# Two halves of the small products in the extra bank, around the other products of a position

## What is computed

```python
h = take(L0_tok_W.T, x)                          # embedding, vocabulary 4360
h = h + toeplitz_mixer(layernorm(h), ...)        # FFT convolution, gates
h = h + product_key_attention(layernorm(h), ...) # 8 heads, see below
h = h + attention(layernorm(h), Wq, Wk)          # softmax(q k / 8) @ x, one head
h = h + moe(layernorm(h), ...)                   # 8 experts, top 2, exact gelu
```

```python
k = einsum('bnhk,bnhkd->bnhd', kv_scores, keys_table[ind])
v = einsum('bnhk,bnhkd->bnhd', kv_scores, values_table[ind])
attn = softmax(where(causal, einsum('bihd,bjhd->bhij', q, k), neg), -1)
out = einsum('bhij,bjhd->bhid', attn, v) @ Wo
```

## Time and profile before

| | |
|---|---|
| median of three executions | 3286.44 us |
| profiled execution, span | 3919.1 us |
| profiled execution, mean granted TensorE clock | 0.869 |
| PE busy | 2986.0 us, 76% |
| DVE busy | 2791.8 us, 71% |
| ACT busy | 2037.7 us, 52% |
| POOL busy | 2052.1 us, 52% |

### The profile page before, as it was taken

How to read it: one execution, slowest core, us unless ns; L and a number is a source line. 1 busy time by engine, 2 the same in 40 slices (tenths; PEclk the granted TensorE clock), 3 DMA queues, 4 the chain that set the end, 5 groups by cost and what they waited for, 6 DMA issues and landing times. The chain is left out here.

```text
span 3919.1 us, 39389 instructions
## 1 busy us (share of the span) xinstructions
PE 2986.0 (76%) x9782; PEld 1393.2 (36%) x9782; DVE 2791.8 (71%) x9999; ACT 2037.7 (52%) x4498; POOL 2052.1 (52%) x2095
## 2 busy tenths in 40 slices
PE   4861667868786768878787878787878878787888
PEld 2430222424333323334333433333333433333443
DVE  7678777777777777777768786767768887864423
ACT  3231544555555655556555655555555755555522
POOL 3011666566666666565656655555656565655300
PEclk7985777989788989999889989888988989998999
DMA  1001121212121212111111111121211111111000
GB/s 37 22 8 52 45 66 43 59 46 58 48 58 48 58 48 59 45 53 51 54 50 48 56 45 55 41 57 44 58 45 52 53 51 48 47 56 42 23 3 3
DMA packets 85626, 179.86 MB, mean 46 GB/s; under 512 B 40177, under 2 KB 41107, under 8 KB 85398
## 3 DMA queue, kind: packets, MB, share of 16 engines
q0 software_dynamic: 66560, 135.40, 13.2%
q1 hardware_dynamic: 18838, 41.94, 3.4%
HBM read 176.15 MB, written 1.05 MB: 45 GB/s over the span
## 5 line engine op out<-in xcount | busy, mean ns | idle before, releaser
L1356 POOL DMA_INDIRECT mx_G<-in_kv_table,mx_slot_i x2048 | 1998.7, 976 | 1388.0 <-issue 605.7
L1384 PE MATMUL mx_acc<-mx_W,mx_table 128*128 128x512 f32 x2048 | 1179.6, 660 | 3.4 <-ACT mx_kvT L1586 3.2
L1743 DVE SCALAR_TENSOR_TENSOR mx_W<-mx_D,mx_W 128x512 f32<-128x512 f32 x1024 | 698.5, 682 | 352.7 <-ACT mx_W L1579 257.9
L1579 ACT ACTIVATE mx_W<-mx_D 128x512 f32<-128x512 f32 x1024 | 607.5, 594 | 525.0 <-remote 235.1
L1647 ACT ACTIVATE mx_GT<-mx_G,mx_slot_w 128x128 f32<-128x128 f32 x2048 | 759.1, 495 | 3.9 <-DVE mx_KVs L1960 1.9
L1374 PE MATMUL mx_D<-mx_U,mx_pick_b 96*128 96x512 bf16 x1024 | 434.3, 424 | 117.6 <-remote 53.8
L1384 PEld LDWEIGHTS mx_acc<-mx_W,mx_table 128*128 128x128 f32 x2048 | 437.4, 215 | 214.9 <-issue 130.4
L1603 ACT ACTIVATE mx_PT<-mx_area 128x512 f32<-128x512 f32 x480 | 246.7, 516 | 455.1 <-remote 145.2
L1396 PE MATMUL mx_O<-mx_PT,mx_KVs 128*65 128x512 f32 (+3 forms) x768 | 333.2, 517 | 130.7 <-ACT mx_OT L1595 86.7
L1410 PE MATMUL mx_area<-mx_KTa,mx_QTa 64*128 64x512 f32 (+3 forms) x384 | 202.9, 613 | 248.0 <-DVE mx_mx_part L1978 83.0
L1960 DVE TENSOR_REDUCE mx_KVs<-mx_GT 128x128 f32<-128x2048 f32 x128 | 292.0, 2281 | 7.5 <-ACT mx_GT L1647 7.3
(11 more groups left out here) (382 smaller groups left out, 4439.9 us busy)
## 6 DMA issues: line engine op xcount, KB each, us to landing
mx_table<-in_kv_dense SPq DMA_DIRECT2D x64, 512.0 KB
mx_G<-in_kv_table,mx_slot_i POOLq DMA_INDIRECT x2048
tz_table<-in_c_dft SPq DMA_DIRECT2D x1, 2048.0 KB
tz_table<-in_c_idft SPq DMA_DIRECT2D x8, 256.0 KB, 2.6
out_h<-mx_xc SPq DMA_DIRECT2D x4, 256.0 KB
mx_G<-in_c_pick SPq DMA_DIRECT2D x1, 528.0 KB
st_h<-in_tok_W,em_ids POOLq DMA_INDIRECT x32
st_keys<-in_pk_keys SPq DMA_DIRECT2D x1, 512.0 KB, 3.8
```

What stands on the lines that cost most here:

```text
L1356: pool.indirect_dma_start(G[g % RING][:, r, :], None, a["kv_table"], bass.IndirectOffsetOnAxis(slot_i[n % 2][:, k, r:r + 1], 0))\
L1384: pe.matmul(acc[:, :], table[:, tile, :], W[c % TILE_RING][:, :], start=(tile == 0), stop=(tile == TILES - 1)).then_inc(applied, 1)
L1579: act.activation(W[c % TILE_RING][:, :], D_ps[c % 3][:, :], ACT.Exp).then_inc(p_done, 1)
L1743: dve.scalar_tensor_tensor(W[c % TILE_RING][:, :], D_ps[c % 3][:, :], 0.0, W[c % TILE_RING][:, :], ALU.is_ge, ALU.mult).then_inc(w_done, 1)
```

## The change

Five of the uses of the extra bank (U, post, KK, neg, Y) are cut in two. The two waits and the first half of the transposes or products move into `begin_extra`, which runs ahead of the position's other products; the second half stays where it was, and it alone tells that the bank is ready. Where the position has a weigh or an area product, the first half stands behind `apply_dense` and ahead of those; where it has neither, it stands between `score_dense` and `apply_dense`. The other uses keep their place whole. No instruction is added or taken away.

```diff
+            def begin_extra(key):
+                kind, n = key[0], key[1]
+                if kind not in ("U", "post", "KK", "neg", "Y"):
+                    return
+                pe.wait_ge(x_taken, cnt.x[key])
+                if kind == "U":
+                    pe.wait_ge(pc_ready, STEPS * n + key[2] // 2 + 1)
+                    turn_split(key, (0, 1))
...
+            def project_heads(key, parts):
+                head = key[1] % HP + HP * key[2]
+                for j in parts:
+                    last = pe.matmul(X_ps[:, j * (D + 1):(j + 1) * (D + 1)], OT[:, j * P:(j + 1) * P], o_w[:, head, :],
+                                     start=True, stop=True)
+                return last
...
             def fill_extra(key):
-                pe.wait_ge(x_taken, cnt.x[key])
+                if kind not in ("U", "post", "KK", "neg", "Y"):
+                    pe.wait_ge(x_taken, cnt.x[key])
...
                 if kind == "U":
-                    pe.wait_ge(pc_ready, STEPS * n + key[2] // 2 + 1)
-                    flat = X_ps[:, :].bitcast(BF16)
-                    for g in range(4):
...
+                    last = turn_split(key, (2, 3))
...
+                key = cnt.x_at.get(divmod(q, SLOT))
                 late = c % TILES == 0
+                early = bool(area_uses(q - 2)) and area_uses(q - 2)[0] in cnt.weigh or bool(area_uses(q))
+                if key is not None and not early:
+                    begin_extra(key)
                 if 0 <= c < PAIRS * SLOT and not late:
                     apply_dense(c)
+                if key is not None and early:
+                    begin_extra(key)
                 for use in area_uses(q - 2):
                     if use in cnt.weigh:
                         weigh(use)
```

More of the change, by code:

```diff
@@ L1467, in idle_products @@
                               skip_group_check=True)
+            def begin_extra(key):
[6 more added lines that the diff above has]
+                    turn_split(key, (0, 1))
+                if kind == "post":
+                    pe.wait_ge(acc_taken, 2 * n + key[2] + 1)
+                    turn_sums((0, 1))
+                if kind == "KK":
+                    pe.wait_ge(kv_ready, NB * n + 4 * key[2] + 4)
+                    turn_keys(key, (0, 1))
+                if kind == "neg":
+                    if key[2] == 0:
+                        pe.wait_ge(scores_taken, cnt.scored["S", n, 1, 3] + 1)
+                    else:
+                        pe.wait_ge(max_done, 2 * n + 2)
+                    turn_maxima(key, (0, 1))
+                if kind == "Y":
+                    pe.wait_ge(o_taken, cnt.o["ST", n, key[2], key[3]] + 1)
+                    project_heads(key, (0, 1))
@@ new lines, in turn_split, with turn_sums @@
+            def turn_split(key, parts):
+                flat = X_ps[:, :].bitcast(BF16)
+                for g in parts:
+                    for e in range(2):
+                        at = (2 * g + e) * P
+                        last = pe.transpose(flat[0:96, at:at + P], PC[:, key[2] % 2 * 2 + e, g, :, :].rearrange("p a c -> p (a c)"),
+                                            ident_b[:, :])
+                return last
+            def turn_sums(parts):
+                for j in parts:
+                    last = pe.transpose(X_ps[:, j * P:(j + 1) * P], kvT[:, j * P:(j + 1) * P], ident[:, :])
+                return last
@@ new lines, in turn_keys, with turn_maxima @@
+            def turn_keys(key, parts):
+                for j in parts:
+                    last = pe.transpose(X_ps[:, j * P:(j + 1) * P], KV[key[1] % 2][:, 4 * key[2] + j, 0:2 * D], ident[:, :])
+                return last
+            def turn_maxima(key, parts):
+                for j in parts:
+                    last = pe.matmul(X_ps[0:D + 1, j * P:(j + 1) * P], mx[:, key[2], j:j + D + 1], ident[:, :],
+                                     start=True, stop=True)
+                return last
@@ L1483, in fill_extra @@
                 if kind == "U":
-                    pe.wait_ge(pc_ready, STEPS * n + key[2] // 2 + 1)
-                    flat = X_ps[:, :].bitcast(BF16)
-                    for g in range(4):
[L1487 to L1490, removed]
+                    last = turn_split(key, (2, 3))
                 if kind == "post":
-                    pe.wait_ge(acc_taken, 2 * n + key[2] + 1)
-                    for j in range(4):
-                        last = pe.transpose(X_ps[:, j * P:(j + 1) * P], kvT[:, j * P:(j + 1) * P], ident[:, :])
+                    last = turn_sums((2, 3))
                 if kind == "KK":
-                    pe.wait_ge(kv_ready, NB * n + 4 * key[2] + 4)
-                    for j in range(4):
-                        last = pe.transpose(X_ps[:, j * P:(j + 1) * P], KV[n % 2][:, 4 * key[2] + j, 0:2 * D], ident[:, :])
+                    last = turn_keys(key, (2, 3))
                 if kind == "QQ":
@@ L1502, in fill_extra @@
                 if kind == "neg":
[L1503 to L1509, removed]
-                if kind == "Y":
[L1511 to L1515, removed]
+                    last = turn_maxima(key, (2, 3))
+                if kind == "Y":
+                    last = project_heads(key, (2, 3))
                 if kind in ("l1x", "l2x"):
@@ L1566, in _ @@
                         fill_area(use)
-                if divmod(q, SLOT) in cnt.x_at:
-                    fill_extra(cnt.x_at[divmod(q, SLOT)])
+                if key is not None:
+                    fill_extra(key)
                 if 0 <= c < PAIRS * SLOT and late:
```

## The result

| | before | after |
|---|---|---|
| median of the runs | 3286.32 us (4 runs, 3283.16 to 3289.22) | 3309.51 us (4 runs, 3304.64 to 3315.03) |
| ratio, 95% interval | | 1.0062 [1.0049, 1.0075] |

A forecast was written before the change was run, and what follows sets the result against it. Neither engine fills the span: TensorE and VectorE take turns as the bound. Terms 6.9 + 6.9 + 0 + 3.2 + 0 - 3.6 = 13.4 us on 3286.4 gave 3299.8, or 3300 us; range 3275 to 3325 us.

The forecast's parts named there:

- position 6: Second U: the apply would wait for the previous U's copy, 0.86 us in 8 slots without other products; +6.9 us.
- position 5: First U: the apply would wait for VectorE's adds, 0.86 us in 8 slots without other products; +6.9 us.
- position 4: Y: TensorE would wait 0.65 us for the copy of sim in 7 slots, but covered; 0, uncovered 4.6 us.
- position 38: U behind the U of position 37: the score area would start about 0.2 us later in 16 slots; +3.2 us.
- position 26: Half of neg can fill a score area's wait for maxima, 7 us in all, but TensorE has time; 0.
- order within Y: Two runs of four have two short first steps in place of one, 0.06 us for 64 uses; -3.6 us.
- positions 7 to 15: Positions 8, 12 and 13 lie where VectorE is behind; 0, bounded by 13.8 us if ScalarE is late at 13.
- the first half would find the bank free (0): Position 5 with a weigh or area: VectorE's adds end before the weigh starts, so no wait; 0.
- the delay is covered by VectorE's backlog: Position 4: VectorE comes to read Y only after it is through, so TensorE's delay costs 0.
- rival of filled waits: First halves run in area products' waits for maxima at positions 26 and 38; -10.7 us, 3276 us, chance 19%.
- ScalarE's lateness: Copies at 4, 13 and 38 come after the new place, applies and areas lose cover; 3310 to 3343 us, chance 10%.
- The covered waits: At positions 5 and 6 TensorE's lost time comes out of waits it has anyhow; 3286 up to 3293 us, 26%.

The follow-up runs named there:

- cut_456: The changed kernel with uses cut only in positions 4, 5 and 6, whole in the old place elsewhere; 3308.67 us, 1.0059 of before.
- waits_first: The changed kernel with the waits moved ahead but all products of a use in their old place; 3310.12 us, 1.0059 of before.
- second profile of before: The kernel before, unedited, run and profiled again; 3289.38 us, ratio 1.0000, span 3290.5 us.
- cut_5_beside: The changed kernel with uses cut only in position 5 of slots with a weigh or area product there; 3298.81 us, 1.0025 of before.
- cut_beside: The changed kernel with uses cut only in positions with a weigh or area product, whole elsewhere; 3303.07 us, 1.0043 of before.
- cut_alone: The changed kernel with uses cut only in positions without a weigh or area product, whole elsewhere; 3295.74 us, 1.0020 of before.
- cut_dense: The changed kernel with uses cut only in positions 42 to 63, whole in the old place elsewhere; 3286.79 us, 0.9995 of before.
- u_later: The kernel before with the two U of positions 5 and 6 moved whole to 6 and 7; 3279.29 us, 0.9965 of before.
- u_later_all: The kernel before, uses whole, with U of 5 and 6 at 6 and 7, U of 38 at 39, post of 40 at 41; 3282.42 us, 0.9972.

## Why the prediction was right, and where it was right by luck

The forecast was 3300 us, by TensorE's stalls behind moved waits in positions 4 to 6. The time is 3309.5 us, and that mechanism is shown three times: by place (cut_456), by part (waits_first) and in the idle time of the groups. That the number came near is partly luck, as the terms show. The distances, 14 slots, beside the sum's terms for 16:

```
term                     predicted   measured (distances)
position 6                   +6.9        +7.5
position 5                   +6.9       +16.6
position 4                    0          +7.7
position 38                  +3.2        +2.3
position 26                   0         -10.0 (27 to 36: +4.7)
order within Y               -3.6        -2.2 (three Y of four)
positions 7 to 15             0         -11.3
```

**Position 6.** Nearly right. In the slots without other products it lost 5.4 us in 7 of the 8, where 7 x 0.86 = 6.0 were priced; where it took 1.8 us before (slots 2, 3 and 6), it takes 2.7. That nothing is paid in slots where the position has other products was only nearly right too: 2.0 us (3.2 to 3.7 in some).

**Position 5.** The step "the first half would find the bank free (0)" where there is a weigh or an area failed. It rested on one slot, in which the adds ended 0.19 us ahead of the weigh, and that slot was from the disturbed profile. The row itself held the warning: that apply takes 2670.68 - 2668.97 = 1.71 us to the next start, twice the 0.86 that was priced, so the slack was that of an apply at half clock. In the second profile of before, the same slot 12 (PE, then DVE):

```profile
2236.02 1.02 PE L1384 MATMUL mx_acc<-mx_W,mx_table 128*128 128x512 f32 x2
2236.88 1.02 PE L1396 MATMUL mx_O<-mx_PT,mx_x 128*65 128x512 f32 x2
...
2236.85 0.85 DVE L2007 SCALAR_TENSOR_TENSOR st_h<-mx_X,mx_rz,st_h 128x64 f32<-128x64 f32 x4
```

Here the adds end at 2237.70, 0.82 us after the weigh starts. In all eight slots of this kind they end after that place, by 0.2 to 3.4 us. In slot 11 of before, PE from the apply on:

```profile
2068.57 1.02 PE L1384 MATMUL mx_acc<-mx_W,mx_table 128*128 128x512 f32 x2
2069.43 1.02 PE L1440 MATMUL mx_area<-mx_KTl,mx_QTl 128*128 128x512 f32 x2
2070.37 0.65 PE L1489 MATMUL mx_X<-mx_ident_b,mx_PC 128*96 128x128 bf16 x8
```

and of after (PE, then DVE: the last add of the heads):

```profile
2079.10 1.02 PE L1384 MATMUL mx_acc<-mx_W,mx_table 128*128 128x512 f32 x2
2081.04 0.42 PE L1501 MATMUL mx_X<-mx_ident_b,mx_PC 128*96 128x128 bf16 x4 [0.92 <-DVE st_h L2053]
2081.30 1.08 PE L1440 MATMUL mx_area<-mx_KTl,mx_QTl 128*128 128x512 f32 x2
2082.22 0.39 PE L1501 MATMUL mx_X<-mx_ident_b,mx_PC 128*96 128x128 bf16 x4
...
2080.14 0.85 DVE L2053 SCALAR_TENSOR_TENSOR st_h<-mx_X,mx_rz,st_h 128x64 f32<-128x64 f32 x4
```

The adds end at 2080.14 + 0.85 = 2080.99, which is 1.89 us after the start of the apply. The area product, whose data are ready, ran under the adds before; now it starts at 2081.30 in place of some 0.9 us after the apply. The distance of the position grows by 0.9 to 1.1 us in six of the seven such slots (2.5 to 3.6 and 3.2 to 4.2) and by 2.1 us in slot 14, 8.2 us in all, and cut_5_beside prices it at +7.5 us at the end. The slots without other products lost 8.4 us in seven, where 6.0 were priced. This is the step that made the sum too small, and the prediction had its size as the upper bound: 16 x 0.86 = 13.8 us against 6.9.

**Position 4.** The step "the delay is covered by VectorE's backlog" failed. The prediction priced it at 0.65 us without the cover; in the slots without other products, five of six lost 0.8 and one 1.1 us, and the others lost 2.5 us together, most of it in slot 10. In slot 5 of after, PE (for the earlier trace rows):

```profile
1030.35 0.38 PE L1374 MATMUL mx_D<-mx_U,mx_pick_b 96*128 96x512 bf16 x1
1031.27 0.66 PE L1524 MATMUL mx_X<-mx_o_w,mx_OT 65*128 65x65 f32 x4 [0.54 <-ACT mx_S L1661]
1031.77 1.08 PE L1384 MATMUL mx_acc<-mx_W,mx_table 128*128 128x512 f32 x2
1032.68 0.56 PE L1524 MATMUL mx_X<-mx_o_w,mx_OT 65*128 65x65 f32 x4
...
1036.17 0.62 PE L1501 MATMUL mx_X<-mx_ident_b,mx_PC 128*96 128x128 bf16 x4 [2.72 <-DVE st_h L2053]
1036.59 2.02 PE L1384 MATMUL mx_acc<-mx_W,mx_table 128*128 128x512 f32 x2
1038.40 0.64 PE L1501 MATMUL mx_X<-mx_ident_b,mx_PC 128*96 128x128 bf16 x4
1038.83 0.64 PE L1374 MATMUL mx_D<-mx_U,mx_pick_b 96*128 96x512 bf16 x1
```

The order is the one foretold: score, half, apply, half. Y's two halves and the apply between them are pushed back by the wait for sim, and the next wait on VectorE's adds takes 2.72 us in either kernel (2.79 before).

**Which slots count.** The sum charged the slots without other products. By the windows these lose nothing at the end where no last-layer product stands in the slot at all (slots 1 to 5), and the loss comes from slots 6 to 15. Over all 13 undisturbed profiles slots 1 to 5 take 822.2 to 824.8 us, whatever was cut or moved, and slots 6 to 15 take 1715.7 to 1746.7. Of the eight slots charged at positions 5 and 6, five (1 to 5) cost nothing, and the slots set at 0 cost the most: cut_beside loses 10.9 us in slots 6 to 15. So 13.4 us were near the 20 measured partly because slots that cost nothing were charged in place of those that cost. That is luck. cut_alone loses 4.8 of its 6.4 us in slots 6 to 15: of the ten, slots 6, 9 and 13 have no other product in positions 4 to 6, and lose 10.9 us there, of which 4.8 reach slot 16. The other 1.6 us are within the noise. That slots 1 to 5 absorb the stall because TensorE has 17% to spare there, against 9% in the others, is argued from the busy shares; no run tested it.

**Positions 26, 38 and the dense stretch.** At 26 half of neg did fill the wait: 10.0 us in 14 slots, where 7 were priced in 16. Not all of that is the half, since the position also falls by 4.9 us in cut_456, where neg is whole. VectorE was the late one there, as argued, and ahead of the longer areas TensorE waits 15.7 us more (88.9 to 104.6). So the rival of filled waits had its mechanism right, but not the way to the end. ScalarE's lateness did not come: position 38 lost 2.3 us. The covered waits hold for slots 1 to 5 alone. Positions 42 to 47 grew by about 5 us in after, for which the sum has no term: 2.2 us in slots 6 to 15, nearly all the late copy ahead of 46 (cut_dense, above), and the rest in slots 2 to 5, where it doesn't reach the end. In Y's term, 0.06 x 64 makes -3.8 us and not -3.6; nothing hangs on it.

## What to carry to other kernels

On an engine that works in order, price a wait that is moved ahead by the ready work that it is moved past, in every kind of position, and measure the slack (the new place less the releaser's end) over many slots, at the full clock, before a term is set to 0: here one slot with 0.19 us of slack, at half clock, stood for eight with none. If a small product stalls on its data, move it back whole to a position where the data are ready (u_later, -12.0 us); to divide it and send one half ahead moves the stall onto the large products (+20 us). A local loss reached the end here only in slots 6 to 15, where the engine was busy 91%, so sum by slots as well as by positions.

## What the runs showed of the hardware

One profiled execution of an unchanged kernel had a span of 3919.1 us with idle holes on all engines, and another 3290.5 us, where nothing is put down to "remote". A profile whose span is 19% above the timed runs should be taken again before waits are read from it.

The stretch behind the last score product of the pairs holds the same 742 products in every kernel here, and its time goes by the clock granted in it: 214.3 and 214.4 us at 0.98, 216.4 to 216.6 us at 0.96, 220.6 and 222.1 at 0.94, 222.7 to 224.3 at 0.93, 224.6 and 224.9 at 0.92. Runs with and without the cut stand at both ends (after 214.3, cut_456 224.9; u_later 216.5, u_later_all 222.1). So one profile can be off by 10 us through the clock alone, half of what the change costs.

After the stall of 2.7 us in slot 5, the granted clock was half. These are a stretch of 3.1 us ahead of that stall and one behind it, after:

```profile
1030.30:1033.40 3.10, 2.56 (x13) 1.37 (x11) 3.10 (x19) 2.38 (x7) 2.49 (x3) 1.00 0.25 62
1036.10:1039.20 3.10, 3.03 (x11) 1.54 (x11) 1.58 (x12) 0.13 (x1) 2.19 (x4) 0.52 0.17 42
```

The apply ahead took 1032.68 - 1031.77 = 0.91 us to the next start, and the one behind 1038.40 - 1036.59 = 1.81 us: the clock stood at 2.4 and then at about 1.2 GHz. Before has that too (0.50 there), but its apply, 1037.90 to the next start at 1039.61, ran beside ScalarE's copy of U, while the moved one stands between the two halves that the copy waits for. So an apply behind such a stall takes 1.8 us and not 0.86; the prediction's own rows had it (1.71 us in the earlier trace rows) and its sum didn't. That the loss doubles with it isn't shown: positions 5 and 6 of this slot together grew by 0.6 us (4.91 + 2.99 to 5.75 + 2.72).
